# A transformer block with routed experts: the order of three queues ahead of the first expert tiles

## The reference

```
x = x + 0.5 * ffn(layernorm(x))
x = x + attention(layernorm(x))
x = x + 0.5 * ffn(layernorm(x))

ffn(x):  xn = layernorm(x) * gamma + beta
  abel   = gelu(xn @ abel_w + abel_b)
  logits = xn @ moe_gate_w + moe_gate_b          # 8 experts, the best 2 of each token
  w      = softmax of the two best logits
  h_e    = gelu(xn @ ew1[e] + eb1[e])            # 128 -> 256
  moe    = sum over the two e of w_e * (h_e @ ew2[e] + eb2[e])
  moe    = moe @ expm(gens[0]) @ expm(gens[1]) @ expm(gens[2])
  gate   = sigmoid([abel, moe] @ gc_w + gc_b)
  return x + abel * (1 - gate) + moe * gate
```

## Time and profile before

| | |
|---|---|
| median of three runs | 861.92 us (859.76 to 862.28) |
| profiled execution | 863.43 us, its span 861.7 us |
| PE, busy | 676.8 us (79%) |
| VectorE, busy | 578.5 us (67%) |
| GpSimd, busy | 488.8 us (57%) |
| ScalarE, busy | 413.5 us (48%) |
| chain that ended last | PE 46%, DVE 24%, issue 10%, SP's queue 5% |
| mean granted clock of PE | 0.922 of full |

### The profile page before, as it was taken

The page is one execution under the profiler, slowest core; times in us unless marked ns, Lnnn a source line. Parts: engine busy times, 40 slices in busy tenths (PEclk is TensorE's granted clock), DMA queues, the critical chain, the costliest instruction groups (busy, mean ns, idle before and its releaser), DMA issues.

```text
span 861.7 us, 18401 instructions
## 1 busy us (share of the span) xinstructions
PE 676.8 (79%) x5103; PEld 504.6 (59%) x5103; DVE 578.5 (67%) x2057; ACT 413.5 (48%) x931; POOL 488.8 (57%) x588
## 2 busy tenths in 40 slices
PE   1568637996969897999989999999996938768960
PEld 0458636885965564655656556565653428757950
DVE  3678867888739873867767677676773205687565
ACT  2246204563630564564655646556554725645540
POOL 2567783062205673668868687463545544567772
PEclk9669958999989998999999999999998969999895
DMA  8412343673254313023040230302200145233365
GB/s 209 163 42 91 104 108 77 154 190 84 73 144 130 80 26 92 2 70 85 22 120 17 72 83 16 93 13 63 55 14 30 32 121 160 80 84 97 105 216 166
DMA packets 86703, 77.15 MB, mean 90 GB/s; under 512 B 14497, under 2 KB 72492, under 8 KB 86444
## 3 DMA queue, kind: packets, MB, share of 16 engines
q1 hardware_dynamic: 71288, 51.22, 22.8%
q0 software_dynamic: 8800, 18.93, 7.5%
q10 hardware_dynamic: 6516, 5.82, 2.7%
HBM read 36.79 MB, written 30.34 MB: 78 GB/s over the span
## 4 chain that ended last, share of the span: by engine, by line
PE 46%; DVE 24%; issue 10%; SPq 5%; DMA 4%; ACT 4%; POOL 3%; ACTq 2%; DVEq 1%; POOLq 0%
PE bank L2356 8%; PE bank L2284 8%; PE bank L2331 7%; PE bank L2186 5%; PE pair L2127 3%; PE bank L2200 3%; DVE mx L1833 2%; DVE mx L1835 2%; SPq L565 2%; DVE arena L1706 2%; POOL y_rows L895 2%; DVE stat L1335 1%; DVE arena L1753 1%; PE pair L2379 1%; DMA y_rows<-arena 1%
## 5 line engine op out<-in xcount | busy, mean ns | idle before, releaser
L1252 ACT ACTIVATE arena<-bank 128x512 f32<-128x512 f32 x320 | 186.1, 601 | 173.8 <-PE bank L2331 171.0
L926 POOL TENSOR_SCALAR_AFFINE_SELECT arena<-arena 128x256 f32<-128x256 f32 (+1 forms) x192 | 94.5, 516 | 124.8 <-ACT arena L1252 124.7
L2284 PE MATMUL bank<-kZ,qT 128*128 128x512 f32 (+3 forms) x512 | 149.1, 358 | 18.9 <-DVE mx L1836 6.6
L2331 PE MATMUL bank<-qT,kZ 128*128 128x512 f32 (+3 forms) x512 | 155.7, 375 | 2.2 <-DMA qT<-mT_zero 1.5
L1191 ACT ACTIVATE arena<-bank,hidden_bias 128x128 f32<-128x128 f32 x320 | 91.1, 368 | 91.7 <-PE bank L2186 88.7
L2284 PEld LDWEIGHTS bank<-kZ,qT 128*128 128x128 f32 x512 | 87.2, 196 | 66.9 <-DVE mx L1836 19.3
L1833 DVE TENSOR_REDUCE mx<-bank 128x1 f32<-128x512 f32 x128 | 87.2, 681 | 50.3 <-PE bank L2258 49.7
L2186 PE MATMUL bank<-arena 128*128 128x128 f32 x640 | 92.7, 290 | 24.0 <-DVE arena L1753 12.3
L895 POOL DMA_INDIRECT y_rows<-arena x80 | 79.9, 999 | 47.3 <-DVE arena L1706 28.1
L2356 PE MATMUL bank<-arena,vA 128*9 128x512 f32 (+3 forms) x1024 | 94.3, 448 | 15.4 <-issue 6.1
L2200 PE MATMUL bank<-w_rot,arena 128*128 x640 | 98.0, 290 | 7.1 <-ACT arena L1191 7.0
(11 more groups left out here) (275 smaller groups left out, 1222.4 us busy)
## 6 DMA issues: line engine op xcount, KB each, us to landing
arena<-z_rows SPq DMA_DIRECT2D x160, 66.0 KB
qT<-parts SPq DMA_DIRECT2D x42, 128.0 KB
kZ<-parts SPq DMA_DIRECT2D x168, 32.0 KB
y_rows<-arena SPq DMA_DIRECT2D x20, 264.0 KB, 3.5
beside_kZ<-y_rows SPq DMA_DIRECT2D x7, 528.0 KB, 6.6
z_rows<-in_spare SPq DMA_DIRECT2D x4, 528.0 KB, 6.5
z_rows<-in_spare SPq DMA_DIRECT2D x32, 66.0 KB
w<-in_ew SPq DMA_DIRECT2D x2, 1024.0 KB, 6.5
```

Of the source, the lines that this page charges most:

```text
L926: g_.affine_select(out=cut, in_=cut, compare_op=ALU.is_ge, fill=0.0, base=0, pattern=[[0, 2], [0, blocks], [1, P]], channel_multiplier=-1) ...
L1252: a_(dst, src, ACT.Exp).then_inc(exp_ok.sem, 1)
L2284: mm(outp, qT[u][:, t, query_tile * P:(query_tile + 1) * P], kZ[u][:, h, 0:keys], start=start, stop=False, skip_group_check=(kind != "full"))
L2331: return mm(outp, kZ[u][:, h, lo:lo + P], qT[u][:, t, lo:SEQ], start=start, stop=True, skip_group_check=(kind != "full"))
```

## The change

SP's program in the prologue is reordered: the zeroing of run 0's gaps comes after the third abel store instead of after the eighth; quads 0 to 3 are loaded after the sixth store, ahead of the last two stores and of the wait for the transposes of w2; quads 4 and 5 follow that wait as before. The three bias transfers leave SP's queue: ScalarE issues them at the start of its `experts(0)`, after waiting for `bias_parts`. On VectorE the first run's table is made in the loop's round n = 3 instead of after the loop; the second run's count and table are made beside pair 1 of the first expert stage instead of before and after `fold_rotation`; the two `y_places` move from pairs 2 and 4 to pairs 4 and 6.

```diff
@@ SyncE @@
             sp.wait_ge(cst, ZEROED + 1)
-            for g in range(CH):
+            for g in range(3):
                 keep_abel(g)
             zero_gaps(0)
+            for g in range(3, CH - 2):
+                keep_abel(g)
+            for q in range(X_TOP):
+                load_x(0, q)
+            for g in range(CH - 2, CH):
+                keep_abel(g)
             sp.wait_ge(w2T_pe, 4)
-            for q in range(X_BUFS):
+            for q in range(X_TOP, X_BUFS):
                 load_x(0, q)
-            sp.wait_ge(bias_parts, 1)
-            for r in range(3):
-                sp.dma_start(expert_bias[r:r + 1, :, :], b2_parts[0:E, r, :]).then_inc(expert_bias_in, 16)
             zero_gaps(1)
@@ ScalarE, experts(layer) @@
                 act.wait_ge(ld_bias, 16 * NJ)
+                if layer == 0:
+                    act.wait_ge(bias_parts, 1)
+                    for r in range(3):
+                        act.dma_start(expert_bias[r:r + 1, :, :], b2_parts[0:E, r, :]).then_inc(expert_bias_in, 16)
                 x_out_(0)
                 x_out_(1)
@@ VectorE, the loop over n = 2 to 7 @@
                 keep_squares(range(3 * n - 5, 3 * n - 3))
                 if n == 2:
                     small_parts()
-            make_table(0)
-            count_rows(1)
+                if n == 3:
+                    make_table(0)
             fold_rotation()
-            make_table(1)
@@ VectorE, beside_experts(layer, p) @@
                 if layer == 0:
-                    if p == 2:
+                    if p == 1:
+                        count_rows(1)
+                        make_table(1)
+                    if p == 4:
                         y_places(0)
-                    if p == 4:
+                    if p == 6:
                         y_places(1)
```

## The result

| | before | after |
|---|---|---|
| median, 15 runs of each | 862.61 us (859.76 to 867.35) | 859.79 us (854.97 to 864.75) |
| profiled execution | 863.43 us, span 861.7 | 860.09 us, span 858.3 |
| mean granted clock of PE | 0.922 | 0.927 |

A forecast was written before the change was run, and what follows sets the result against it. SP's queue order was taken to set PE's expert start within a PE and DVE chain. Of 16.6 us, 6.2 survive the memsets, less 1.5 for restart: 861.92 - 4.7 = 857.2 us; 8-in-10 range 851.0 to 861.0.

The forecast's parts named there:

- Start: First expert stage: PE may turn its first tile at 117 instead of 133.60, 16.6 us sooner.
- the ready weights: End of the folding: rotated weights ready between 116.0 and 118.4 us, taken as 117.0.
- the table in round n = 3: Squaring loop: the first run's table is paid in full, 3.4 us, plus 1.5 for PE's clock; squarings end 4.9 later.
- up to 2.4: Folding: without the idle time ahead, PE's clock may be whole and give back up to 2.4 of 9.1 us.
- Queues: Prologue: SP's loads issued by 112, bias rows landed from ScalarE's queue by 115.4 to 117.1, hidden behind the weights.
- The collision: First expert stage: copy 8 stands behind GpSimd's memsets until 137.8; third down product about 138.3, leaving 6.2 of 16.6 us.
- holds for any weights-ready time from 116 on: First expert stage: the 6.2 us left was said to depend on the memsets' end, not on the start.
- The third rival: Memsets in the first expert stage: VectorE copies pass after each memset, 8.0 us saved, 853.9 us; chance 0.10.
- The restart: After PE's standstill, near 138 us: clock at half for 3.1 us, costing 1.5 us.
- the place computations: First expert stage, each moved by two pairs: worse place put at nothing, bounds 0 and 2.2 us.
- The second rival: Later first expert stage: DVE has no room, both place computations fully paid, 2.5 us saved, 859.4 us; chance 0.11.
- own range: Main case's total time: 854.8 to 859.4 us, by which copy is caught and how slowly the clock returns.

The follow-up runs named there:

- bias_only: The kernel before the change, with only the three bias transfers moved to ScalarE's queue; 861.28 us, ratio 0.9984.
- bias_split_wait: The kernel before, with bias transfers on ScalarE's queue and key memsets in semaphore-waiting pieces; 957.71 us, ratio 0.9846, in a later series (kernel before 972.47).
- split_wait: The changed kernel with each key memset cut in 8, each piece waiting on a semaphore for the one before; 848.92 us, ratio 0.9844.
- places: The changed kernel with the two place computations beside pairs 3 and 4 instead of 4 and 6; 858.17 us, ratio 0.9951.
- warm: The changed kernel with 92 identity transposes on PE ahead of its fourth up product, within the stall; 859.5 us, ratio 0.9969.
- split: The changed kernel with each key memset cut in 8 pieces, back to back; 859.2 us, ratio 0.9958.
- tt_table: The changed kernel with weight copies 8 to 18 and the second run's table conversion as two-input operations; 857.86 us, ratio 0.9923.
- tt_copies: The changed kernel with VectorE's weight copies 8 to 18 of the first expert stage as two-input maximums; 859.4 us, ratio 0.9951.

## Why the prediction was right, and what in it was off

**Start.** Predicted 117.0 for the ready weights, measured 115.5 (112.80 + 2.68), and the first turn 116.29. The product that ends the squarings was over at 109.1 where 109.3 was said: the table in round n = 3 is paid there (PE's clock falls to 0.50 in it, as estimated). The clock then was 1.00 through the whole folding, 109 to 116, and it took 6.4 us in place of 9.1: 2.7 given back, more than the "up to 2.4", so that 115.5 lies outside the 116.0 to 118.4. In this execution the term doesn't matter, as the text said, because the end of the memsets fixes the outcome.

**Queues.** SP's loads were out at 113.0 (112 was said), the bias rows at 114.9, within its 115.4 to 117.1 for landing less 1.1. ScalarE's issue costs 0.71 us apiece, SP's 0.76. Neither is waited for: right. That the loads had to be moved for it was taken on trust. bias_only shows they hadn't (in the later series of bias_split_wait one quad's turn does wait for them, 1.48 us); the prediction read "24 loads, then bias rows" and credited SP's order as a whole, where one of its two halves carried the start.

**The collision.** The prediction's central step, confirmed down to the copy: copy 7 slips in, copy 8 is caught and ends at 137.2, the third down product goes at 137.99 (138.3 said). Left of the start: 6.5 us (6.2 said). The memsets ended 0.56 us sooner than taken, at 137.07, and PE went 0.92 us after them where the sum had 0.67. split_wait puts the price of the collision at 10 us, by taking it away. But that it "holds for any weights-ready time from 116 on" is wrong: with the weights ready at 116.3 (places) and 116.5 (warm) VectorE was still in the table when the memsets came, the table's step was caught, and 2.0 and 2.9 us of lead were left at quad 3 in place of 4.8. By the forecast's own 117.0 the table would have been over at 126.5, nearer to this case than the measured 125.75. That copy 8 was the one caught is luck in part.

**A rule of the Trainium skill.** The third rival let VectorE in after one memset. That was a reading of what the Trainium skill says (SBUF — State Buffer, "Who interferes with whom"): a lock held for the whole of one instruction. Its chance had been kept low because the earlier trace rows showed three memsets in a row without a change of hands; split now shows two dozen. VectorE got in between two of GpSimd's instructions only in the kernels with waiting pieces, where there is a gap.

**The restart.** 1.5 us said, from 3.1 us at half clock. The clock was back only after some 4.7 us. From the third down product to the turn of quad 3 PE needs 4.26 us without idling, and needed 2.51 before: 1.75. warm, which takes it away, wins 1.0 to 1.4. So this term was too small by a quarter microsecond; the larger remainder of the collision made up for it (6.5 less 1.75 is the 4.8 seen, where 6.2 less 1.5 was said).

**The term that was mis-sized: the place computations.** The prediction "put their worse place at nothing, bounds 0 and 2.2". They cost 0.95 us, the lead lost between quads 5 and 6. VectorE's 1.4 us of places (148.62 to 150.0) delay the copy and the evacuation two pairs on. From 153.77 to 154.38 it frees the banks that PE's down product at 154.63 waits for. By the order of PE's program the register reads for the next quad stand behind that product in its queue, and they lie bare: 1.05 us of "issue" ahead of 157.01, in a window where PE does nothing and VectorE is busy throughout. (That it is the reads which fill it follows from this order; they have no row of their own. In split and warm the profile names ScalarE for the same wait, but in split its last work ended at 156.33, 0.85 us before PE went on.) The second rival (VectorE has no room) was thus half right. The delay was passed on only where PE's own register reads follow. places puts it back to 4.87.

**The sum.** 17.3 at the start, 6.5 after the memsets, 4.8 after the restart (4.7 said), 3.8 after the places. In the profiled executions 3.3 arrive, by the ratio 3.1. The last half microsecond is lost after the first expert stage and its place wasn't sought. Against the 4.7 of the forecast the place computations are the larger part of the miss in this execution. (In the forecast's "own range" the lower end, 854.8, doesn't follow from its terms: 6.6 off 861.92 is 855.3.)

**The wider spread.** The changed kernel's runs cover 9.8 us, those before 7.6, which is little to go by with 15 of each. The traces of places and warm (the table's step is caught) and tt_table (copy 7), with memsets that start 0.7 to 0.9 us and a VectorE that comes 1.1 to 1.3 us later than in the changed kernel's (copy 8), suggest a reason: VectorE's program around 126 us meets the memsets at another place each time, and the place decides how much is lost (quad 3 is turned at 142.25 with copy 8 caught, 143.66 with copy 7, 144.19 and 145.01 with the table's step). That the spread of the changed kernel itself comes from this is argued, not shown, for only one of its executions has a trace.

## What to carry to other kernels

Before moving work forward, look at what else lies in the stretch that it moves into: here 17 us of earlier start met a wall of 10 us that had cost the first expert stage nothing where it was. Long GpSimd instructions that no one is waiting for should have gaps, a semaphore wait between pieces is enough, if VectorE copies within the memory run beside them; shorter pieces alone did nothing here. When an order of queues is changed in several parts, try the smallest alone: three small transfers on another queue gave 16.7 of the 17.3 us by which PE's first turn came sooner, though not the first up product, which still waited for the tables on VectorE.

## What the runs showed of the hardware that was not expected

- GpSimd's memsets kept VectorE's copy out over some 22 boundaries when they followed at once: 24 pieces, one every 0.47 us, held it for 10.79 us. A semaphore wait between them lets it in, at 0.28 to 0.69 us a copy, and GpSimd needs 14.35 us in place of 11.26.
- An operation of VectorE can be caught up to 1 us ahead of the memset's recorded start (126.43 and 126.74, memsets 127.42 and 127.37). GpSimd's operation before it, `rstd_g`, takes 3.3 to 3.4 us in place of 2.93 in the three traces where this happened by 0.6 us or more, so it is slowed too. "The one that starts first" can't be read from these records.
- Size doesn't protect: a step of 128x56 that takes 0.18 us alone was held for 11.45. The form does: a copy written as the maximum of a tensor with itself takes 0.42 us (0.28 as a copy) and ran through the memsets. So did a reduction from memory to memory (0.29 us, tt_copies), although it has one input, and operations that read PE's banks. Not every form was tried.
- A held instruction counts as busy. VectorE shows 9.71 us busy of 11 from 126 us on, for one copy of 0.28 us of work; only the timeline, with the mean of the same form elsewhere, gives it away.
